# Cross-scan layers: VectorE forms the third injected tile in three groups of each turn, in place of GpSimd

## What is computed

```python
def _selective_scan(u, delta, A, Bs, Cs, Ds, delta_bias):
    delta = jax.nn.softplus(delta + delta_bias[None, :, None])
    def step(h, inp):
        dt, ut, bt, ct = inp
        dA = jnp.exp(dt[..., None] * A_k[None])
        dBu = dt[..., None] * bt[:, :, None, :] * ut[..., None]
        h = dA * h + dBu
        y = jnp.einsum('bkdn,bkn->bkd', h, ct)
        return (h, y)
...
xs = jnp.concatenate([x_hwwh, jnp.flip(x_hwwh, axis=-1)], axis=1)
x_dbl = jnp.einsum('bkdl,kcd->bkcl', xs, x_proj_weight)
...
y = y * jax.nn.silu(z)
return jnp.einsum('bhwd,cd->bhwc', y, out_proj_weight)
```

## Time and profile before

| | |
|---|---|
| median of 3 runs | 3706.26 us (3704.75 to 3708.18) |
| profiled execution, its own time | 3695.08 us |
| its span, first to last instruction | 3693.3 us |
| VectorE busy | 2993.3 us |
| GpSimd busy | 2825.9 us |
| TensorE busy | 2781.2 us |
| ScalarE busy | 2038.8 us |
| TensorE's mean granted clock | 0.804 |

### The profile page before, as it was taken

How to read it: one execution, slowest core, us unless ns; L and a number is a source line. 1 busy time by engine, 2 the same in 40 slices (tenths; PEclk the granted TensorE clock), 3 DMA queues, 4 the chain that set the end, 5 groups by cost and what they waited for, 6 DMA issues and landing times. The chain is left out here.

```text
span 3693.3 us, 27850 instructions
## 1 busy us (share of the span) xinstructions
PE 2781.2 (75%) x6084; PEld 633.8 (17%) x6084; DVE 2993.3 (81%) x1944; ACT 2038.8 (55%) x2278; POOL 2825.9 (77%) x1212
## 2 busy tenths in 40 slices
PE   5768777887888788335767676688778787887887
PEld 2111111111111112111111122111111111111111
DVE  1889898988998896675988923999889888988893
ACT  3566565656565665314565525656565656656562
POOL 1889989998998897003665614999889989998993
PEclk9787887878887878657888778788787878878788
DMA  2655646563755554103443405475546555564652
GB/s 54 158 132 140 150 119 155 136 153 85 177 131 137 128 141 107 29 0 87 121 115 82 102 0 117 122 165 136 135 115 150 140 129 125 142 157 111 156 135 59
DMA packets 140402, 437.16 MB, mean 118 GB/s; under 512 B 33429, under 2 KB 34139, under 8 KB 139915
## 3 DMA queue, kind: packets, MB, share of 16 engines
q1 hardware_dynamic: 140234, 435.53, 49.0%
HBM read 307.50 MB, written 6.82 MB: 85 GB/s over the span
## 5 line engine op out<-in xcount | busy, mean ns | idle before, releaser
L865 POOL TENSOR_TENSOR L_read<-L_state,L_c_rows 128x1024 f32<-128x1024 f32 x768 | 1799.3, 2362 | 120.0 <-DVE L_state L973 78.7
L656 PE MATMUL L_y_ps<-L_read,L_fold 128*64 128x512 f32 x3072 | 1241.8, 908 | 340.8 <-POOL L_read L865 310.8
L796 ACT ACTIVATE L_work_ps<-L_delta,L_a_neg 128x1024 f32<-128x1024 f32 x256 | 286.3, 1118 | 647.7 <-DVE L_state L973 647.6
L852 POOL TENSOR_TENSOR L_state<-L_du,L_b_rows 128x1024 f32<-128x1024 f32 x256 | 605.2, 2364 | 25.3 <-POOL L_read L865 3.2
L973 DVE TENSOR_TENSOR_SCAN L_state<-L_decay,L_work_ps 128x1024 f32<-128x1024 f32 x256 | 585.2, 2286 | 26.7 <-DVE L_work_ps L954 1.9
L973 DVE TENSOR_TENSOR_SCAN L_state<-L_work_ps,L_state 128x1024 f32<-128x1024 f32 x256 | 581.1, 2270 | 18.2 <-POOL L_state L852 15.7
L796 ACT ACTIVATE L_decay<-L_delta,L_a_neg 128x1024 f32<-128x1024 f32 x512 | 584.5, 1142 | 16.7 <-issue 6.9
L973 DVE TENSOR_TENSOR_SCAN L_state<-L_decay,L_row_ps 128x1024 f32<-128x1024 f32 x256 | 585.3, 2287 | 8.8
L954 DVE TENSOR_TENSOR L_work_ps<-L_du,L_row_ps 128x1024 f32<-128x1024 f32 x256 | 314.3, 1228 | 269.6 <-issue 142.9
L656 PEld LDWEIGHTS L_y_ps<-L_read,L_fold 128*64 128x64 f32 x3072 | 189.2, 159 | 1264.8 <-POOL L_read L865 832.8
L1503 POOL TENSOR_TENSOR L_read<-L_state,L_c_rows 128x1024 f32<-128x1024 f32 x96 | 236.7, 2466 | 167.4 <-DVE L_state L1609 142.8
(11 more groups left out here) (322 smaller groups left out, 2971.7 us busy)
## 6 DMA issues: line engine op xcount, KB each, us to landing
L_c_rows<-L_bc_dram SPq DMA_DIRECT2D x580, 256.0 KB, 4.0
L_b_rows<-L_bc_dram SPq DMA_DIRECT2D x580, 256.0 KB, 4.2
L_delta<-L_delta SPq DMA_DIRECT2D x204, 256.0 KB, 5.9
L_du<-L_du SPq DMA_DIRECT2D x140, 256.0 KB, 6.1
L_du<-L_u SPq DMA_DIRECT2D x64, 256.0 KB, 6.0
L_bc_dram<-L_dbl SPq DMA_DIRECT2D x40, 128.0 KB, 3.4
L_delta<-L_delta_a SPq DMA_DIRECT2D x16, 256.0 KB, 4.3
L_du<-L_du_a SPq DMA_DIRECT2D x16, 256.0 KB, 5.1
```

What stands on the lines that cost most here:

```text
L656: m = nc.tensor.matmul(y_ps[i * BLK:(i + 1) * BLK, c, :], fold[:, :], y_half(t, o, i), start=first, stop=last, skip_group_check=True)
L796: nc.scalar.activation(to[:, :], delta2[:, d * NBLK + c, :], ACT.Exp, scale=a_neg[:, o * 2 + d, c, p:p + 1]).then_inc(decay_ready, 1)
L852: nc.gpsimd.tensor_tensor(state[:, last, :], du2[:, d * NBLK + last, :], b_rows[:, g % 2, :], ALU.mult).then_inc(injected_c, 1)
L865: nc.gpsimd.tensor_tensor(read[:, t % READS, :], state[:, t % STATES, :], c_rows[:, g % 2, :], ALU.mult).then_inc(multiplied, 1)
```

## The change

A table `DVE_THIRD` names three groups of each turn: 10, 13 and 14 in even turns, 8, 10 and 12 in odd ones. In these GpSimd leaves the third injected tile out, and VectorE forms it (`inject_third`) ahead of the injected tile of c1, while `row_ps` still holds the B row. It waits on the same count `multiplied` as GpSimd did, and adds to the same count `injected_c`.

```diff
--- before.py
+++ after.py
@@ -324,6 +324,7 @@
                  ("log", 1): 28, ("one", 1): 29, ("less", 1): 30, ("relu", 1): 32, ("exp", 2): 33, ("log", 2): 34,
                  ("one", 2): 35, ("less", 2): 36, ("relu", 2): 38}]
 POOL_GAP = [{29: 0, 36: 1, 39: 2}, {22: 0, 28: 1, 34: 2}]
+DVE_THIRD = ((10, 13, 14), (8, 10, 12))
 ACT_SIDES = ("u", "bc", "dt", "sum", "z", "cent", "var")
 SILU_AT, RSTD_AT, Y_AT, ADD_AT = 10, 29, 3, 33
 SKIP_AT = (1, 2, 3)
@@ -856,7 +857,7 @@
                 number = turn.number
                 for t in range(NT):
                     g = t // NBLK
-                    if t % NBLK == 0:
+                    if t % NBLK == 0 and g not in DVE_THIRD[turn.r]:
                         inject_c(number, g)
                     pool.wait_ge(scanned, number * NT + t + 1 + SCAN0)
                     if t % NBLK == 0:
@@ -955,6 +956,15 @@
                 dve.wait_ge(injected, (number * GROUPS + g) * 2 + c + 1 + INJECT0)
                 return to
 
+            def inject_third(number, g):
+
+                d, last = g // NP, NBLK - 1
+                if g % NP == 0:
+                    dve.wait_ge(du2_in[d * NBLK + last], (number + 1) * PER_BLOCK)
+                dve.wait_ge(multiplied, (number * GROUPS + g) * NBLK + MULT0)
+                nc.vector.tensor_tensor(state[:, last, :], du2[:, d * NBLK + last, :], row_ps[:, :],
+                                        ALU.mult).then_inc(injected_c, 1)
+
             def turn_of(turn):
                 number = turn.number
                 for t, (d, p, c) in enumerate(tiles):
@@ -962,6 +972,8 @@
                     for at, key, i in turn.sides:
                         if at == t - DVE_LAG and key[0] in ("sum", "cent", "shift", "out"):
                             finish_side(turn, key, i)
+                    if c == 1 and g in DVE_THIRD[turn.r]:
+                        inject_third(number, g)
                     if c < 2:
                         by, fed = decay[:, c, :], inject_tile(number, t)
                     else:
```

## The result

The changed kernel takes 3737.26 us (median of 4 runs, 3734.37 to 3744.69), the kernel before beside it 3705.51 (3703.53 to 3708.18). The ratio is 1.0088, 95% interval [1.0071, 1.0106]: **slower by 31.8 us**. The forecast was slower, 3745, range 3712 to 3780.

A forecast was written before the change was run, and what follows sets the result against it. No engine was taken as full; VectorE (81% busy) and GpSimd (77%) nearly so, with waits between them deciding. 8 x 2.6 + 8 x 2.2 = 38.4 us on the 3706.26 us median gave 3744.7, say 3745 us, range 3712 to 3780.

The forecast's parts named there:

- GpSimd gains nothing: Group 8, odd turn: GpSimd's last read still ends at 699.6; in general a changed group costs GpSimd 0 to 1.2 us.
- the chain from VectorE over ScalarE's decay and copy of u to the side bank: Odd turn after group 8: VectorE's 2.2 us delay passes through ScalarE, whose copy of u frees the side bank.
- +2.6 us per odd turn: Delays from groups 8, 10 and 12, followed through the odd turn shown, lengthen each odd turn by 2.6 us.
- the next side matmuls and the first product for du (709.78) start about 2.1 late: Odd turn, after group 8: the late copy of u moves the first product for du from 709.78 to 711.9.
- +2.2 us per even turn: Delays from groups 10, 13 and 14, followed through the even turn shown, lengthen each even turn by 2.2 us.
- Only the read of c0 comes earlier, and I find nothing that waits for it: In each changed group, only GpSimd's read of the group's first tile comes earlier, and nothing was found to profit.
- a fifth of 38.4 us: Lower end of the range: most delay is absorbed by the rings, leaving 6 us, 3712 us.
- VectorE's occupancy: Rival: all work added to VectorE, the busiest engine, lengthens the path, 58 us, 3764 us; chance 0.12.
- GpSimd's saving: Rival: GpSimd sets the pace and its saving comes through in odd turns, 56 us less, 3650 us; chance 0.06.
- Idle time swallows it: Rival: VectorE's own waits per turn, 12 and 28 us, absorb added work and delays; within 0.2%, 3706 us; chance 0.08.
- Delays pile up through slower hand-overs: Rival: delays accumulate, also through a TensorE held up more, 5 us a turn, 3786 us; chance 0.12.

The follow-up runs named there:

- experiment 1: The change made in the odd turns alone, against the kernel before; 3733.54 us, ratio 1.0076.
- experiment 8: The change made in group 8 of the odd turns alone, against the kernel before; 3728.54 us, ratio 1.0071.
- experiment 5: Odd turns: VectorE forms the third tile in an idle buffer, read there by the scan, without waiting for GpSimd's read; against the kernel before, 3719.68 us, 1.0045.
- experiment 9: The change in odd turns, plus one zero product on TensorE ahead of tiles 25, 26 and 27; 3724.01 us, 1.0052 against the kernel before.
- experiment 2: The change made in the even turns alone, against the kernel before; 3699.49 us, ratio 0.9983.
- Experiment 11: The kernel before plus zero products on TensorE ahead of tiles 33, 34 and 43 of even turns; 3686.12 us, 0.9946 against the kernel before.
- Experiment 6: As experiment 5, and the same in groups 13 and 14 of even turns, group 10 keeping the wait; 3719.39 us, 1.0044 against the kernel before.
- experiment 10: The kernel before plus zero products on TensorE ahead of odd tiles 25, 26 and 27; 3730.64 us, 1.0060 against the kernel before.
- experiment 4: Odd turns: GpSimd keeps its third tile, VectorE forms an unused copy without the wait; 3705.25 us, 1.0000 against the kernel before.
- Wait alone: Odd turns: GpSimd keeps its third tile, VectorE only waits where it would have formed it; 3711.82 us, 1.0017 against the kernel before.

## Why the prediction was right and where it was wrong

**The mechanism: right.** VectorE waits for GpSimd's read ahead of the third product, the inject and scan of c1 stand behind it, and GpSimd, 108 us lighter, waits for scans for 118.5 us more (all its idle time together grew by 150, as forecast). The product takes 1.214 us where 1.21 was taken. In group 8 each instruction stands within 0.11 us of where the text put it. Also right: "GpSimd gains nothing", and the chain from VectorE over ScalarE's decay and copy of u to the side bank.

**"+2.6 us per odd turn": too small.** It measured 4.5 in the profiles and 3.5 by the median of experiment 1. The step that fell short is "the next side matmuls and the first product for du (709.78) start about 2.1 late": it passed a delay on through TensorE at a fixed duration. With the change TensorE pauses ahead of the product for 1.2 to 1.5 us in every odd turn, and then runs it partly at the lower clock level, 3.3 to 4.2 us instead of 2.85 (up to 5.44 in experiment 8). What bears this out: experiment 5, where the wait is gone, the pause and the low level stay, and 16 us stay with them; and experiment 9, where filling the pause restores 2.84 us and 9.5 us of time. What share of the 28 us is the clock is not settled: the fillers cost time of their own, and in experiment 5 GpSimd's earlier reads changed other hand-overs too. How the loss is spread over groups 8, 10 and 12 is not settled either (experiment 8).

**"+2.2 us per even turn": wrong.** It measured 0.2 in the profiles, and a gain of 6 us in all by experiment 2. The sentence that failed is "Only the read of c0 comes earlier, and I find nothing that waits for it". In group 13 VectorE does wait as forecast, and in group 14 the product comes behind side products without a wait (timeline of VectorE, even turn, groups 13 and 14):

```profile
3132.66 1.22 DVE L965 TENSOR_TENSOR L_state<-L_du,L_row_ps 128x1024 f32<-128x1024 f32 x1 [1.56 <-POOL L_read L866]
...
3144.26 1.21 DVE L965 TENSOR_TENSOR L_state<-L_du,L_row_ps 128x1024 f32<-128x1024 f32 x1
```

but the turn is not longer for it. The first even sum product takes 4.5 us at 0.62 in seven of the eight even turns of before and in one of the eight here. TensorE stood still for the same 1.95 us right ahead of it in both kernels, so the pause alone does not set the level (the first row is of before, the second of the changed kernel):

```profile
3077.03 1.96 PE L631 MATMUL L_side_ps<-L_y_a,ident 128*128 128x512 f32 x2 [1.95 <-ACT L_delta L711]
```

```profile
3115.78 1.12 PE L632 MATMUL L_side_ps<-L_y_a,ident 128*128 128x512 f32 x2 [1.95 <-ACT L_delta L712]
```

The product is here

```profile
3115.78:3118.62 2.84, 2.84 (x8) 1.12 (x10) 1.48 (x1) 2.01 (x2) 2.76 (x2) 1.00 0.02 9
```

(a window of the changed kernel). Over the six even turns that are not the first of a layer its mean record goes from 0.87 to 0.66 us and the last sum product's from 0.87 to 0.71, but the fourth one's from 0.61 to 0.78; over all six sum products of all eight even turns it is 0.71 before and 0.67 after. That this pays for the delay is argued from these records, and not shown. Experiment 11, which raises the same products in the kernel before and gains 19 us, makes it likely. Experiment 6, where the first of them is raised in every even turn and the time stays that of experiment 5, makes it less so. No run isolates it, since even turns with unchanged code moved by up to 22 us between these profiles (1413.2 us before, 1435.7 in experiment 10).

**The sum.** 38.4 us was forecast and 31.8 measured: an odd term too small and an even term too large, which partly cancel. The total is closer than its parts deserve, and that is luck. Two figures of the prediction do not hold by its own terms or rows: a fifth of 38.4 us is 7.7 and not 6, so the lower end would be 3714; and the even turn that was worked on, 182.5 us, was taken for all, whose mean is 176.7.

**The rivals.** VectorE's occupancy (3764): fell by experiment 4, which tested the odd turns. GpSimd's saving (3650): fell, since read c1 waits 2.45 us in group 8. Idle time swallows it (3706): true of the even turns, and of the work alone, not of the change. Delays pile up through slower hand-overs (3786): its size did not come, but its clause on a TensorE "that is held up more" was nearest to what the odd turns show. Wait alone (+6.5) and work alone (0) do not sum to both together (+28). I read this as two delays that must meet before TensorE is held up enough to run the product low; that reading was not tested further, and the 1.95 us pauses of the even turns at either level show that it is more than the length of one pause.

## What to carry to other kernels

Moving work from an engine that gets its ordering for nothing to one that must wait for it can cost what is queued behind that wait, so price the wait and the work apart, and then together, since here neither alone shows the loss. On a ring of short hand-overs a late TensorE product can also be a slower or a faster one: look at the granted clock over exactly that product, before and after. Zero products that fill such a pause can be worth more than moving the work (0.9946 here). In the kernel before they helped where products ran low (experiment 11) and hurt where the product ran high already (experiment 10), and they must be placed anew after each other edit.

## What the runs showed of the hardware

- The same float32 side product takes 2.84 or 2.85 us at a granted clock of 1.00, 3.98 at 0.71, 4.54 at 0.62 and 5.44 at 0.52. Fillers that raised it at a few of these products went with a gain of 19 us (experiment 11), where 29 us of added VectorE work moved the kernel by nothing (experiment 4).
- The length of the last pause does not set the level: behind the same 1.95 us the product ran at 0.62 in the kernel before and at 1.00 in the changed one, and in one odd turn of experiment 5 it ran at 1.00 after a pause of 2.15 us with 3.8 us of work between.
- A VectorE product of 128x1024 float32 takes 1.214 us with one operand in PSUM and one in SBUF, whether it writes SBUF or PSUM (1.209), and 1.711 with both in SBUF beside GpSimd's reads; three of these went from 7.03 to 8.03 us, the one that overlaps the product to 3.38.
